# Scores between two halves of a projection, and factors between two halves of a product

## The chip, the cores and the metric

The kernel runs on one core of a Trainium2 chip. The core's engines are TensorE (PE in the profile), VectorE (DVE), ScalarE (ACT) and GpSimd (POOL), with SyncE (SP), which issues most of the DMAs. Each engine works through its own list of instructions in order and waits for the others on semaphores. The metric is the device time of one launch in microseconds, the median over several runs.

## What is computed

One decoder layer over `x` of (4, 1024, 256): a Hyena operator, cross-attention to a context of 64 rows per batch, and a gated feed-forward part with quantised weights, each followed by a residual addition and a layer norm.

```python
def hyena(u):                                   # after a projection and a depthwise convolution of 3 taps
    for n in range(2):
        y = irfft(rfft(v, n=2 * L) * rfft(h[n], n=2 * L))[..., :L]
        v = y * x[:, n]
    return v.transpose(0, 2, 1) @ w_out.T + b_out

def xattn(x_q, x_kv):                           # 16 heads of 16, 64 context rows
    q, k, v = x_q @ W_q.T + b_q, x_kv @ W_k.T + b_k, x_kv @ W_v.T + b_v
    attn = softmax(einsum('bhqd,bhkd->bhqk', qh, kh) / 4)
    return einsum('bhqk,bhkd->bhqd', attn, vh) @ W_out.T + b_out

x = layernorm(x + hyena(x))
x = layernorm(x + xattn(x, ctx))
x = layernorm(x + bitlinear(silu(bitlinear(x, w_gate)) * bitlinear(x, w_up), w_down))
```

## The kernel before

The program has two blocks, one after the other, with a barrier of all engines between them.

**The filter stage** (`hyena`) goes through the four batches. Transforms are matrix products on TensorE; for a batch `b` there are two of them, `u = 2b` and `u = 2b + 1`. For each, TensorE writes the spectrum into banks in four steps (L389, L390, L405), VectorE multiplies two banks per step by the filter (`products`, L1171 and L1172, eight steps `j` with two pairs of buffers that alternate), and GpSimd adds the real and imaginary parts into `spec_y` (`add_products`, L904 and L905; the last step is VectorE's own). A product of VectorE may overwrite its buffer once GpSimd has read what it held two steps ago (`y_ready`), and TensorE may write a bank again once VectorE has read it (`prod_done`). Then TensorE transforms back (L437, L446), and VectorE combines and gates (`level_one`, `level_two`).

The output of batch `b - 1` is finished inside batch `b`: VectorE adds the projected output to the rows (`add_residual`, L1286, in two groups of four tiles, which also gives the sums of the rows), ScalarE squares (`squares`, L780), GpSimd turns sums and squares into factors (`norm_factors`, L960 to L966: four small operations per group), ScalarE scales (`norm`, L787), and SP stores the group, waits for the store, and loads the next batch's group in its place. In the last batch `norm_factors(b - 1)` stands on GpSimd ahead of `add_products(u + 1)`. The rows of the last batch itself stay on chip (`x_tok`) and are normalised at the start of attention.

**Attention** (`attention_and_feed_forward`) works on 32 tiles of 128 rows, in chunks of 4 (`CH`). For tile `j`, TensorE makes the scores of all heads (`scores`, L1668) into `ps_score`, which has one buffer: the scores of tile `j + 1` wait until VectorE has taken the peaks (L2203) and subtracted them (`shift`, L2207) for tile `j`. ScalarE takes exponentials (L1866, two halves), TensorE turns them (`turn_prob`, L1678), ScalarE copies them out (`evac_prob`, L1872). Two tiles together give the sums of the exponentials (`sums`, L1689), VectorE's reciprocal of them (`invert`, L2214), and the weighted values (`values`, L1704). The reciprocals go through DRAM to be spread, GpSimd multiplies, and TensorE projects.

Queries of chunks 0 to 4 come from the filter stage. Those of the chunks 5, 6 and 7 (`Q_EARLY` is 5) are made among the first tiles: TensorE turns the rows (`turn_x`, L1642), ScalarE copies them (`evac_x`, L1848), TensorE multiplies by the weights (`queries`, L1650, two halves of two products into the banks `ps_ctx` and `ps_inv`), ScalarE copies them out (`evac_q`, L1853). Chunks 6 and 7 need the rows of the last batch normalised: squares on ScalarE (`squares_last`, L1839), factors and scaling on GpSimd (`norm_last`, L1984 to L1993), in two halves, after which GpSimd adds the output's bias to the chunks from chunk 0 on (`add_bias`, L2003; it waits for the chunk's rows). At tile 0 VectorE also places the values in pairs (L2187: eight additions of two operands in SBUF) and at tile 1 the keys (L2296: two multiplications of two operands in SBUF).

The order of each engine is written out by hand. TensorE's is the loop over tiles:

```python
turn_x(Q_EARLY); queries(Q_EARLY)
for j in range(TILES_ALL):
    scores(j + 1)
    if j == 2: turn_x(Q_EARLY + 2)
    turn_prob(j)
    if j == 0: turn_x(Q_EARLY + 1)
    if j in (1, 2): queries(Q_EARLY + j)
    if j % 2 == 0 and j >= 2:
        sums(j // 2 - 1)
        if j >= 4: values(j // 2 - 1)
    if j == 3: values(0)
```

## Time and profile before

| | |
|---|---|
| median of 3 runs | 682.93 us (682.90 to 683.15) |
| the profiled execution | 682.95 us, of which the span of the instructions is 681.0 us |
| busy | TensorE 96%, VectorE 90%, ScalarE 56%, GpSimd 54% of the span |
| filter stage | to 431.3 us |
| attention | 431.6 to some 556 us |
| feed-forward | to the end |
| TensorE's granted clock | full, 0.998 over the span |

A line of the timeline is one instruction or a run of equal ones: start and duration in microseconds, engine, line of the kernel, operation, what is written and read, and in brackets how long the engine had been idle before it and who released it. "PE" is a matmul, "SPq" and "POOLq" are issues of DMAs. Matmuls overlap, so the distance of two starts tells more than a duration. All times in this text count from the start of the span.

### The profile page before, as it was taken

To read this page: it belongs to the slowest core of one execution; us is meant where nothing else is said; L and a number is where in the kernel's file an instruction comes from. 1 tells how busy PE (TensorE), PEld (TensorE's weight loads), DVE (VectorE), ACT (ScalarE), POOL (GpSimd) and SP (SyncE) were. 2 spreads that over 40 slices of the span, in tenths; PEclk is the share of its full clock that TensorE was granted. 3 is DMA by queue.
4 is the path that set the end of the run, shared out by engine and by line. 5 is a ranking of instruction groups with operands and counts; after the bars stand their busy time and mean duration, and the time that the engine had idled before them with its cause. 6 is when DMAs were issued, how large, how long until landed. Compare 5 with 4: busy or idle time off the path is not lost. (4 is left out here: it accounts for less than half of the span.)

```text
span 681.0 us, 12462 instructions
## 1 busy us (share of the span) xinstructions
PE 650.6 (96%) x4284; PEld 476.8 (70%) x4284; DVE 611.0 (90%) x1241; ACT 384.5 (56%) x761; POOL 365.1 (54%) x506
## 2 busy tenths in 40 slices
PE   9999999999999999999999999888999999999996
PEld 3588765788747887568887677556777775666664
DVE  4899887999999999999999979748999979999997
ACT  3742157131368503475222634569888886888885
POOL 0633424537235753258451381284577769788786
PEclk9999999999999999999999999999999999999999
DMA  8730055230453446443743057552222221010012
GB/s 310 204 63 1 0 125 105 81 62 7 66 107 69 93 155 62 93 93 63 200 100 87 1 185 98 213 174 80 64 80 79 79 79 33 1 34 32 32 63 94
DMA packets 52680, 60.73 MB, mean 89 GB/s; under 512 B 5416, under 2 KB 46376, under 8 KB 52362
## 3 DMA queue, kind: packets, MB, share of 16 engines
q1 hardware_dynamic: 43498, 40.28, 18.3%
q0 software_dynamic: 8256, 18.86, 16.7%
q10 hardware_dynamic: 864, 0.79, 0.4%
q8 instruction: 35, 0.57, 0.3%
q14 instruction: 27, 0.22, 0.1%
HBM read 33.72 MB, written 11.53 MB: 66 GB/s over the span
## 5 line engine op out<-in xcount | busy, mean ns | idle before, releaser
L747 ACT ACTIVATE yb<-banks 128x256 f32<-128x256 f32 x64 | 24.1, 385 | 137.5 <-PE banks L446 92.3
L437 PE MATMUL banks<-inv_m,spec_y 128*128 128x256 f32 x384 | 85.5, 379 | 0.0
L473 PE MATMUL banks<-xt_in,w_in 128*128 128x512 f32 x192 | 84.5, 594 | 0.2
L437 PEld LDWEIGHTS banks<-inv_m,spec_y 128*128 128x128 f32 x384 | 73.0, 190 | 9.9
L389 PE MATMUL banks<-z_cplx,fwd_m 128*128 128x256 f32 x240 | 71.9, 381 | 3.5 <-DVE prod L1172 3.2
L390 PE MATMUL banks<-z_cplx,fwd_m 128*128 128x256 f32 x240 | 71.4, 379 | 0.0
L473 PEld LDWEIGHTS banks<-xt_in,w_in 128*128 128x128 f32 x192 | 36.1, 190 | 43.0 <-issue 40.2
L389 PEld LDWEIGHTS banks<-z_cplx,fwd_m 128*128 128x128 f32 x240 | 44.9, 190 | 11.8 <-issue 5.2
L390 PEld LDWEIGHTS banks<-z_cplx,fwd_m 128*128 128x128 f32 x240 | 45.6, 190 | 6.2
L904 POOL TENSOR_TENSOR spec_y<-prod 128x256 f32<-128x256 f32 x35 | 25.4, 726 | 42.0 <-DVE prod L1172 41.2
L2203 DVE TENSOR_REDUCE peak<-ps_score 128x16 f32<-128x1024 f32 x32 | 38.9, 1215 | 8.7 <-PE ps_score L1668 8.7
L1901 ACT ACTIVATE silu<-ps_score,gate_back 128x1024 f32<-128x1024 f32 x32 | 35.6, 1112 | 18.9 <-issue 17.6
L2253 DVE SCALAR_TENSOR_TENSOR w_raw<-ps_score,up_back,silu 128x1024 f32<-128x1024 f32 x32 | 41.0, 1280 | 1.9 <-ACT silu L1901 1.1
L1872 ACT ACTIVATE prob_t<-ps_pt 128x1024 f32<-128x1024 f32 x32 | 32.7, 1022 | 13.3 <-PE ps_pt L1678 13.3
L2207 DVE TENSOR_TENSOR prob<-ps_score,peak 128x1024 f32<-128x1024 f32 x32 | 39.2, 1224 | 1.1
L2258 DVE TENSOR_REDUCE h_peak<-w_raw 128x1 f32<-128x1024 f32 x32 | 39.0, 1220 | 1.1
L1072 DVE SCALAR_TENSOR_TENSOR z_cplx<-turned_c,sums_c 128x512 f32<-128x512 f32 x60 | 39.9, 718 | 0.0
L405 PE MATMUL banks<-z,fwd_m 128*128 128x256 f32 x168 | 38.0, 379 | 0.9 <-issue 0.9
L1866 ACT ACTIVATE prob<-prob 128x512 f32<-128x512 f32 x64 | 36.8, 622 | 1.2 <-DVE prob L2207 0.9
L2030 POOL TENSOR_TENSOR c_t<-xa_t 128x512 f32<-128x512 f32 x16 | 20.4, 1277 | 31.7 <-DMA xa_t<-inv_scratch 25.7
L405 PEld LDWEIGHTS banks<-z,fwd_m 128*128 128x128 f32 x168 | 31.8, 190 | 7.7 <-issue 3.6
L1678 PE MATMUL ps_pt<-ident,prob 128*128 128x128 f32 x256 | 34.8, 279 | 2.1 <-ACT prob L1866 2.1
(311 smaller groups left out, 1704.4 us busy)
## 6 DMA issues: line engine op xcount, KB each, us to landing
x_tok<-in_x SPq DMA_DIRECT2D x8, 512.0 KB, 4.3
x_tok<-in_b_out POOLq DMA_DIRECT2D x8, 512.0 KB, 13.9
inv_scratch<-inv_sum SPq DMA_DIRECT2D x16, 256.0 KB, 2.6
xa_t<-inv_scratch SPq DMA_DIRECT2D x16, 256.0 KB, 2.7
v_t<-left POOLq DMA_DIRECT2D x8, 511.5 KB, 5.2
x_t<-left POOLq DMA_DIRECT2D x8, 511.5 KB, 5.6
xt_in<-in_x_t SPq DMA_DIRECT2D x3, 1024.0 KB, 5.9
x_scratch<-x_tok SPq DMA_DIRECT2D x6, 512.0 KB, 4.1
```

The source lines that it names most:

```text
L389: mm(o, fwd_m[:, at + 2 * half + odd, :], zz[:, 0, :], start=True, stop=False)
L390: last = mm(o, fwd_m[:, at + 2 * half + 2 + odd, :], zz[:, 1, :], start=False, stop=True)
L405: last = mm(bank[:, half * D:(half + 1) * D], fwd_m[:, w + mt, :], z[:, src, mt, :], start=(mt == 0), stop=(mt == MT - 1))
L437: last = mm(bank[:, odd * 2 * P:(odd + 1) * 2 * P], spec_y[:, j + odd, part * D + h * P:part * D + (h + 1) * P], inv_m[:, o:o + 2 * P], st ...
L473: last = mm(proj_pair(b, t)[:, c * 512:(c + 1) * 512], w_in[:, k, TILES[t] * P:(TILES[t] + 1) * P], xt_in[:, k, c * 512:(c + 1) * 512], st ...
L1072: last = stt(z_cplx[:, g, odd], turned_c[:, slot], sign * factor, src[:, :, 0, :], ALU.mult, ALU.add)
L1866: fn(half, half, ACT.Exp, scale=DH ** -0.5).then_inc(exp_done, 1)
L1901: fn(silu[:, i % 2, :], ps_gate[:], ACT.Silu, scale=gate_back[:, i // CH % 2, i % CH:i % CH + 1])\
L2203: nc.vector.tensor_reduce(pk, sc, AX_X, ALU.max).then_inc(peaked, 1)
L2207: tt(prob[:, j % 2, :].rearrange("p (r h n) -> p r h n", r=STRIPS, n=NCTX), sc, pk.unsqueeze(3).broadcast_to([P, STRIPS, HEADS // STRIPS, ...
L2253: stt(hid[:, k, :], ps_up[:], up_back[:, i // CH % 2, k:k + 1], silu[:, i % 2, :], ALU.mult, ALU.mult)\
L2258: reduce(h_peak[:, k:k + 1], hid[:, k, :], AX_X, ALU.max, apply_absolute_value=True)\
```

## The change

There are four edits.

1. In attention, `queries` becomes `query_half(c, i)`, and TensorE's first tiles are written out without the loop: a tile's scores now stand between the two halves of each of the three projections. ScalarE's first tiles are written out to match. The first pair of tiles gets its sums after the scores of tile 5 and its values after the scores of tile 6; VectorE's first `invert` moves from behind tile 3 to behind tile 4.
2. Four of the eight squares of the last batch's rows move from attention to the end of the filter stage on ScalarE (`squares(B - 1, (0,))`, into `row_var`). GpSimd's `norm_last(0)` waits for no squares. ScalarE makes the other four around the first `evac_x`.
3. In the last batch, VectorE's `add_residual(b - 1)` is split: the first group stands ahead of `level_two(u, 1)`, the second behind it as before.
4. In the last batch, GpSimd's factors of the second group stand between the fourth and the fifth of its seven product additions, and no longer ahead of the first.

```diff
@@ ScalarE, end of the filter stage
             evac_queries(4, IB[0:2])
+            squares(B - 1, (0,))
@@ GpSimd, batch()
                 if last_one:
-                    norm_factors(b - 1)
-                add_products(u + 1)
+                    norm_factors(b - 1, (0,))
+                    add_products(u + 1, 0, 4)
+                    norm_factors(b - 1, (1,))
+                    add_products(u + 1, 4)
+                else:
+                    add_products(u + 1)
@@ VectorE, batch()
                     rotations()
+                    if last_one:
+                        add_residual(b - 1, (0,))
...
                     if last_one:
-                        add_residual(b - 1)
+                        add_residual(b - 1, (1,))
@@ TensorE, attention
-            queries(Q_EARLY)
-            for j in range(TILES_ALL):
+            query_half(Q_EARLY, 0)
+            scores(1)
+            query_half(Q_EARLY, 1)
+            turn_prob(0)
+            turn_x(Q_EARLY + 1)
+            scores(2)
+            turn_prob(1)
+            query_half(Q_EARLY + 1, 0)
+            scores(3)
+            query_half(Q_EARLY + 1, 1)
+            turn_prob(2)
+            turn_x(Q_EARLY + 2)
+            scores(4)
+            turn_prob(3)
+            query_half(Q_EARLY + 2, 0)
+            scores(5)
+            query_half(Q_EARLY + 2, 1)
+            sums(0)
+            scores(6)
+            turn_prob(4)
+            values(0)
+            sums(1)
+            values(1)
+            turn_prob(5)
+            for j in range(6, TILES_ALL):
@@ ScalarE, attention
+            squares_last(0, 2)
             evac_x(Q_EARLY)
-            squares_last(0)
-            for j in range(TILES_ALL):
+            squares_last(2, CH)
+            exponentials(0)
+            act.wait_ge(v_ready, 2 * B)
+            evac_q(Q_EARLY)
+            evac_prob(0)
+            exponentials(1)
+            evac_x(Q_EARLY + 1)
+            evac_prob(1)
+            exponentials(2)
+            evac_q(Q_EARLY + 1)
+            exponentials(3)
+            evac_prob(2)
+            evac_x(Q_EARLY + 2)
+            evac_prob(3)
+            exponentials(4)
+            evac_q(Q_EARLY + 2)
+            weight_sum(0, 0)
+            evac_prob(4)
+            evac_context(0)
+            for j in range(5, TILES_ALL):
@@ GpSimd, attention
             def norm_last(g):
-                pool.wait_ge(l_squared, CH * (g + 1))
+                if g:
+                    pool.wait_ge(l_squared, CH)
@@ VectorE, attention
+                if j == 5:
+                    invert(0)
                 shift(j)
-                if j % 2 and 3 <= j < TILES_ALL - 1:
+                if j % 2 and 5 <= j < TILES_ALL - 1:
                     invert((j - 3) // 2)
```

VectorE, attention, from the peaks of tile 3 on. Before (`peak` is a tile's reduction over the scores, `prob` its subtraction, `inv_sum` the reciprocal of a pair of tiles):

```order
L2203 TENSOR_REDUCE peak<-ps_score 128x16 [waits s_mm]
L2207 TENSOR_TENSOR prob<-ps_score,peak 128x1024 [waits pt_mm,peaked]
L2214 RECIPROCAL inv_sum<-ps_inv 128x128 [waits sum_mm]
L2203 TENSOR_REDUCE peak<-ps_score 128x16 [waits s_mm]
L2207 TENSOR_TENSOR prob<-ps_score,peak 128x1024 [waits pt_mm,peaked]
L2203 TENSOR_REDUCE peak<-ps_score 128x16 [waits s_mm]
L2207 TENSOR_TENSOR prob<-ps_score,peak 128x1024 [waits pt_mm,peaked]
L2214 RECIPROCAL inv_sum<-ps_inv 128x128 [waits inv_written,sum_mm]
L2203 TENSOR_REDUCE peak<-ps_score 128x16 [waits s_mm]
```

Now:

```order
L2230 TENSOR_REDUCE peak<-ps_score 128x16 [waits s_mm]
L2234 TENSOR_TENSOR prob<-ps_score,peak 128x1024 [waits pt_mm,peaked]
L2230 TENSOR_REDUCE peak<-ps_score 128x16 [waits s_mm]
L2234 TENSOR_TENSOR prob<-ps_score,peak 128x1024 [waits pt_mm,peaked]
L2241 RECIPROCAL inv_sum<-ps_inv 128x128 [waits sum_mm]
L2230 TENSOR_REDUCE peak<-ps_score 128x16 [waits s_mm]
L2234 TENSOR_TENSOR prob<-ps_score,peak 128x1024 [waits pt_mm,peaked]
L2241 RECIPROCAL inv_sum<-ps_inv 128x128 [waits inv_written,sum_mm]
L2230 TENSOR_REDUCE peak<-ps_score 128x16 [waits s_mm]
```

The first reciprocal moved behind the subtraction of tile 4; the second stays between tiles 5 and 6.

TensorE, attention. Before, from the second half of the last projection on (`ps_ctx<-xa_t` is a half of the projection, `ps_inv<-prob_t` the sums, `ps_ctx<-prob_t` the values, `ps_pt` turned probabilities):

```order
L1650 MATMUL ps_ctx<-xa_t,left 128x512 x2
L1689 MATMUL ps_inv<-prob_t,w_in 32x128 [waits q_evac,pt_evac]
L1689 MATMUL ps_inv<-prob_t,w_in 32x128 x15
L1668 MATMUL ps_score<-w_in,xt_in 128x128 [waits shifted]
L1668 MATMUL ps_score<-w_in,xt_in 128x128 x7
L1678 MATMUL ps_pt<-ident,prob 128x128 [waits exp_done,pt_evac]
L1678 MATMUL ps_pt<-ident,prob 128x128 x3
L1678 MATMUL ps_pt<-ident,prob 128x128 [waits exp_done]
L1678 MATMUL ps_pt<-ident,prob 128x128 x3
L1704 MATMUL ps_ctx<-prob_t,v_pairs 32x256 [waits pt_evac,v_ready,q_evac]
L1704 MATMUL ps_ctx<-prob_t,v_pairs 32x256 x7
```

Now:

```order
L1656 MATMUL ps_ctx<-xa_t,left 128x512 x2
L1695 MATMUL ps_inv<-prob_t,w_in 32x128 [waits q_evac,pt_evac]
L1695 MATMUL ps_inv<-prob_t,w_in 32x128 x15
L1674 MATMUL ps_score<-w_in,xt_in 128x128 [waits shifted]
L1674 MATMUL ps_score<-w_in,xt_in 128x128 x7
L1684 MATMUL ps_pt<-ident,prob 128x128 [waits exp_done,pt_evac]
L1684 MATMUL ps_pt<-ident,prob 128x128 x3
L1684 MATMUL ps_pt<-ident,prob 128x128 [waits exp_done]
L1684 MATMUL ps_pt<-ident,prob 128x128 x3
L1710 MATMUL ps_ctx<-prob_t,v_pairs 32x256 [waits pt_evac,v_ready,q_evac]
L1710 MATMUL ps_ctx<-prob_t,v_pairs 32x256 x7
L1695 MATMUL ps_inv<-prob_t,w_in 32x128 [waits inverted,pt_evac]
```

The scores of tile 6, the turned probabilities of tile 4 and the first pair's values now stand between the sums of the first pair and those of the second.

GpSimd, last batch of the filter stage, from the factors of the first group on. Before (`rstd` and `shift` are factors, `spec_y` the added products):

```order
L963 TENSOR_TENSOR rstd<-rstd,half_neg 128x4 [waits h_floored]
L966 TENSOR_TENSOR shift<-rstd,shift 128x4 [waits raised,h_centred]
L960 TENSOR_SCALAR rstd<-h_row_var 128x4 [waits x1_ready,h_squared]
L961 TENSOR_SCALAR shift<-h_row_sum 128x4
L963 TENSOR_TENSOR rstd<-rstd,half_neg 128x4 [waits h_floored]
L966 TENSOR_TENSOR shift<-rstd,shift 128x4 [waits raised,h_centred]
L904 TENSOR_TENSOR spec_y<-prod 128x256 [waits inv_done,prod_done]
L905 TENSOR_TENSOR spec_y<-prod 128x256
L904 TENSOR_TENSOR spec_y<-prod 128x256 [waits prod_done]
```

Now:

```order
L963 TENSOR_TENSOR rstd<-rstd,half_neg 128x4 [waits h_floored]
L966 TENSOR_TENSOR shift<-rstd,shift 128x4 [waits raised,h_centred]
L904 TENSOR_TENSOR spec_y<-prod 128x256 [waits inv_done,prod_done]
L905 TENSOR_TENSOR spec_y<-prod 128x256
L904 TENSOR_TENSOR spec_y<-prod 128x256 [waits prod_done]
L905 TENSOR_TENSOR spec_y<-prod 128x256
L904 TENSOR_TENSOR spec_y<-prod 128x256 [waits prod_done]
L905 TENSOR_TENSOR spec_y<-prod 128x256
L904 TENSOR_TENSOR spec_y<-prod 128x256 [waits prod_done]
L905 TENSOR_TENSOR spec_y<-prod 128x256
L960 TENSOR_SCALAR rstd<-h_row_var 128x4 [waits x1_ready,h_squared]
L961 TENSOR_SCALAR shift<-h_row_sum 128x4
```

The second set of four small operations moved behind four pairs of additions.

## Rows read from the trace of the kernel before

**Rows 1.** Timeline of the filter stage, VectorE and TensorE around the additions (start, duration, engine, line, operands)

```profile
377.24 0.41 DVE L1286 SCALAR_TENSOR_TENSOR x_tok<-banks,x_tok 128x256 f32<-128x256 f32 x1
377.53 1.91 PE L464 MATMUL banks<-ident,x_t 128*128 128x128 f32 x16
```

**Rows 2.** Timeline, last batch: GpSimd factors, product additions and those waiting for them

```profile
391.45 0.19 POOL L960 TENSOR_SCALAR rstd<-h_row_var 128x4 f32<-128x4 f32 x1
...
393.20 0.73 POOL L904 TENSOR_TENSOR spec_y<-prod 128x256 f32<-128x256 f32 x1
...
394.71 0.69 DVE L1171 TENSOR_TENSOR prod<-banks,spec_h 128x512 f32<-128x512 f32 x1 [2.06 <-POOL spec_y L905]
...
397.45 0.67 PE L389 MATMUL banks<-z_cplx,fwd_m 128*128 128x256 f32 x2 [0.97 <-DVE prod L1172]
...
408.78 0.42 DVE L1210 SCALAR_TENSOR_TENSOR turned_c<-banks,yc 128x256 f32<-128x256 f32 x1 [0.57 <-ACT yc L750]
```

**Rows 3.** Timeline, end of the filter stage and ScalarE around the block boundary

```profile
426.73 0.42 DVE L1286 SCALAR_TENSOR_TENSOR x_tok<-banks,x_tok 128x256 f32<-128x256 f32 x1 [0.53 <-PE banks L493]
...
431.60 0.20 ACT L1832 ACTIVATE table_of<-h_row_sum 128x1 f32<-128x1 f32 x1 [7.30 <-PEq L142]
...
433.95 0.51 ACT L1839 ACTIVATE a_spread_sq<-x_tok,h_row_sum 128x256 f32<-128x256 f32 x1
```

**Rows 4.** Timeline, first tiles of attention, VectorE, ScalarE and TensorE

```profile
435.04 2.54 DVE L2187 TENSOR_TENSOR v_pairs<-left,w_in 64x128 f32<-64x128 f32 x8
...
440.94 1.02 DVE L2296 TENSOR_TENSOR k_pairs<-left,w_in 128x384 f32<-128x384 f32 x2
...
443.89 0.57 ACT L1848 ACTIVATE xa_t<-ps_ctx 128x512 f32<-128x512 f32 x1
...
445.00 1.98 PE L1650 MATMUL ps_ctx<-xa_t,left 128*128 128x512 f32 x4 [0.31 <-ACT xa_t L1848]
...
446.82 1.88 PE L1650 MATMUL ps_inv<-xa_t,left 128*128 128x512 f32 x4
...
449.43 1.23 DVE L2203 TENSOR_REDUCE peak<-ps_score 128x16 f32<-128x1024 f32 x1 [4.17 <-PE ps_score L1668]
...
450.69 1.22 DVE L2207 TENSOR_TENSOR prob<-ps_score,peak 128x1024 f32<-128x1024 f32 x1
...
456.22 0.96 DVE L2214 RECIPROCAL inv_sum<-ps_inv 128x128 f32<-128x128 f32 x1 [4.31 <-PE ps_inv L1689]
```

**Rows 5.** Timeline, tiles 4 to 6 of attention, TensorE and VectorE

```profile
461.07 1.09 PE L1678 MATMUL ps_pt<-ident,prob 128*128 128x128 f32 x8 [0.78 <-ACT prob L1866]
...
462.09 1.08 PE L1689 MATMUL ps_inv<-prob_t,w_in 128*32 128x128 f32 x32
...
462.99 1.05 PE L1704 MATMUL ps_ctx<-prob_t,v_pairs 128*32 128x256 f32 x16
463.24 0.96 DVE L2214 RECIPROCAL inv_sum<-ps_inv 128x128 f32<-128x128 f32 x1 [0.39 <-PE ps_inv L1689]
...
464.76 1.22 DVE L2203 TENSOR_REDUCE peak<-ps_score 128x16 f32<-128x1024 f32 x1 [0.56 <-PE ps_score L1668]
```

**Rows 6.** Costliest groups of the page (busy, mean ns, idle before): exponentials, turned probabilities

```profile
L1872 ACT ACTIVATE prob_t<-ps_pt 128x1024 f32<-128x1024 f32 x32 | 32.7, 1022 | 13.3 <-PE ps_pt L1678 13.3
...
L1866 ACT ACTIVATE prob<-prob 128x512 f32<-128x512 f32 x64 | 36.8, 622 | 1.2 <-DVE prob L2207 0.9
```

**Rows 7.** Timeline of GpSimd and VectorE: products with and without company

```profile
414.78 2.37 POOL L939 TENSOR_TENSOR v_t<-yq,x_odd 128x1024 f32<-128x1024 f32 x1 [7.23 <-DVE yq L1246]
...
416.06 1.23 DVE L1186 TENSOR_TENSOR sums_c<-turned_c 128x128 f32<-128x128 f32 x1
```

**Rows 8.** Timeline of GpSimd in attention: second half of the rows, then biases

```profile
443.03 0.20 POOL L1984 TENSOR_SCALAR l_rstd<-l_var 128x4 f32<-128x4 f32 x1 [2.13 <-ACT a_spread_sq L1839]
...
447.07 2.35 POOL L2003 TENSOR_TENSOR x<-x,w_in 128x1024 f32<-128x1024 f32 x1
```

**Rows 9.** DMA issues from 431 to 437 us: rows of the stream (count, size, median us to landing)

```profile
x<-x_scratch SPq DMA_DIRECT2D x3, 512.0 KB, 4.9
```

More of the change, by code:

```diff
@@ L770, in squares @@
                     act.wait_ge(act_seq, GROUPS * G_OUT * (b + 1) + 1)
-                for g in range(GROUPS):
+                for g in groups:
                     for t in range(G_OUT):
@@ L896, in add_left, with add_products @@
                     .then_inc(conv_done[slot(b, t)], 16)
[L898 to L899 removed]
+            def add_products(u, j0=0, j1=BANKS - 1, first=False, prod=prod):
+                for j in range(j0, j1):
                     pool.wait_ge(prod_done, 8 * u + j + 1)
```

82 lines of the change are left out of this document (29 added, 53 removed).

## The prediction

> **What bounds the kernel now.** I read the busy shares first. TensorE and VectorE are both busy for nine tenths of the span, so no single engine is the bound, and only a place where one waits for the other can pay. I then read the timeline at the places that the diff touches. In the last batch of the filter stage, VectorE stands 2.06 us behind GpSimd's product additions, and TensorE has to wait for VectorE right after [rows 2]. In attention, VectorE stands 4.17 us before the peaks of tile 3 and 4.31 us before its first reciprocal [rows 4]. From tile 6 on it stands for half a microsecond per tile [rows 5], so attention is paced by the loop of scores, peaks and subtraction, and whatever moves tile 6 moves the end of the kernel by as much. So I price two things: when attention starts, and when VectorE takes the peaks of tile 6, at 464.76 before.
>
> **The additions (edit 3)** bring and cost nothing. VectorE is busy without a gap there and does the same work. The first group's four additions, 1.4 us, now delay the gating, which ended at 377.2. TensorE turned the gated rows from 377.53 on [rows 1], but it came from earlier projections, not from waiting, and its last quarter starts 1.4 us later still. Bounds: 0 to +0.1.
>
> **The factors (edit 4).** The second group's four operations take 393.20 - 391.45 = 1.75 us [rows 2]. Without them the first additions start 1.7 us sooner, and so does VectorE's third product, which stood 2.06 us. What TensorE gets is less. Its last quarter of the transform waited 0.97 us for that product [rows 2]; beyond that it is limited by its own matmuls. With the slower first matmul after a wait I take 1.1 us. The 1.75 us come back on GpSimd behind the fourth step, where VectorE's last three products need them. That eats VectorE's own lead, but VectorE has slack behind it: it waits 0.57 us for ScalarE in front of the second and again of the third bank of the back transform [rows 2], and both waits hang on TensorE. From there TensorE is busy up to the end of the block. So the block ends 1.1 us sooner, between 0 and 1.3. The normalised second group is stored some 4 us later. Behind that store stand SP's loads of the last rows and of the weights of attention, and GpSimd's bias DMA. None of the waits at the end of the block was on a DMA: VectorE waited for TensorE's banks [rows 3]. So I price this at nothing and keep it as a rival.
>
> **The squares (edit 2).** Four squares of 0.51 us with the reading of the sum come to some 2.6 us on ScalarE. They can start with the first additions, at 426.73, and ScalarE was idle for 7.30 us ahead of the boundary [rows 3]; they are done at some 430, a microsecond before VectorE. In attention ScalarE loses four squares. Two of the others precede the first copy of the turned rows, which is late by 0.1 us. The price is nothing. But GpSimd's factors now start at 431.9, not behind squares.
>
> **The first tiles (edit 1), worked out in the clock of before.** The second set of four squares, some 2.4 us, is gone from between the probabilities of tile 0 and the exponentials of tile 1, so that the copies of the turned rows of chunk 6 start at some 441.55, not 443.89. The first half projection follows 445.00 - 443.89 = 1.11 later, at 442.7, and the scores of tile 3 stand behind one half, 446.82 - 445.00 = 1.82 later, at 444.5. The peaks start some 0.8 after them, at 445.3, and not at 449.43 [rows 4]: 4.1 us gained at tile 3. Then the chain runs on: subtraction 1.26 later (450.69 - 449.43), exponentials another 1.26 later at 447.8, on ScalarE 1.04 of exponentials, 0.97 for the turned probabilities (both overlap a little with what follows) [rows 6], 1.11 for the copies of chunk 7, on TensorE half a projection (1.82), scores (some 0.65), the other half (1.81), and the first sums start at 455.2. The reciprocal starts 463.24 - 462.09 = 1.15 after them [rows 5], at 456.4, against 456.22 [rows 4]. It is as late as before, but with four tiles subtracted behind it and one more: tile 5 is subtracted at 458.5 to 459.7. A whole tile is gained.
>
> It is given back at the next reciprocal. VectorE's second reciprocal still stands ahead of the peaks of tile 6. It waits for the second sums, and these now stand on TensorE behind the scores of tile 6 (which wait for VectorE's subtraction of tile 5), the turned probabilities of tile 4 and the first pair's values. From the end of that subtraction: 0.07 to release, 0.65 of scores, 462.09 - 461.07 = 1.02, 0.98 of values (a run of 1.05) and 1.15, together 3.9 us [rows 5] in which VectorE does nothing. The reciprocal starts at 463.6, the peaks of tile 6 0.9 later, at 464.46. That is 0.3 us sooner than before, not 4.
>
> **What GpSimd now collides with.** Two rows show a price for company: while GpSimd multiplies for 2.37 us from 414.78, a VectorE operation with both operands in SBUF takes 1.23 us, up to GpSimd's end [rows 7]; that is 417.2, and for 128 columns, where two key products of 384 columns take 1.02 us together [rows 4]. VectorE's eight value additions (2.54 us from 435.04) and two key products (1.02 us) are of this form. Before, GpSimd was waiting for squares or at operations on four columns then. Now its factors and scalings start at 431.9. A half takes 447.07 - 443.03 = 4.04 us [rows 8], so two of its four scalings lie beside the first value additions, and I take 0.95 us for VectorE's two waits. The two halves end at 431.9 + 8.1 = 440.0, with GpSimd's own waits 440.6, and then the bias of chunk 0 follows at once, since its rows land at some 437 (an issue at 432 and 4.9 us [rows 9]). It takes 2.35 us, to 443.0 [rows 8]. VectorE's key products come due at 441.1, and so wait until 443.0. The peaks of tile 2 start at 444.05, those subtracted at 446.5, the scores of tile 3 at 446.55 and not at 444.5. The chain from there on has no slack, so tile 6 is at 464.46 + 2.05 = 466.5: 1.75 us later than before.
>
> The Trainium skill, "SBUF — State Buffer", section "Who interferes with whom", says that a VectorE instruction with two SBUF inputs and a GpSimd instruction that reads SBUF exclude each other: the one that issues second is blocked until the first has ended. The row of 1.23 us agrees with it, and it speaks against this change: with it attention is 1.75 us slower, without it 0.3 us faster.
>
> **The sum.** 682.95 of the profiled execution (0.02 above the median) - 1.1 + 1.75 = 683.6 us.
>
> **The rivals.**
>
> *No block at the key products.* The two times are only half a microsecond apart. If the products come first or GpSimd is late, only the value additions cost, 0.75 us at tile 3: 682.95 - 1.1 + 0.45 = 682.3. Without any company 682.95 - 1.1 - 0.3 = 681.55. For it speaks that GpSimd's start may slip behind VectorE's clearing of `v_pairs`.
>
> *The gap at the second reciprocal does not open* (it hangs on my reading of the order alone) and the tile gained at 458 stays: 464.76 - 462.1 = 2.7 us, less 2.05: 682.95 - 1.1 - 0.65 = 681.2, and 679.1 if nothing collides either. Against it speaks that both waits are written in the order above.
>
> *Slower: the filter stage gives nothing.* Mechanism: the second group's rows are stored some 4 us later, and the bias DMA of the last batch, which is queued behind store and load, lands after VectorE's additions to the second group want it at 428. It decides from 4 to 5 us of delay on. Then the block ends where it did, and 682.95 + 1.75 = 684.7. If instead chunk 1's rows are there when the bias of chunk 0 ends, the second key product is blocked again, by 2.35: 682.95 - 1.1 + 4.1 = 685.95.
>
> **How the numbers follow.** Forecast 0.46; no block at the key products 0.24, of which half lies at 681.55 or below; no gap at the reciprocal 0.08; no gain in the filter stage 0.14; a second block 0.08. The predicted time is 683.6. The range leaves out the very fast end and the second block: 681.2 to 685.2. A measurement tells some 0.2% (1.37 us) from no change: faster than 681.56 in 0.12 + 0.08 = 0.20, slower than 684.3 in 0.14 + 0.08 = 0.22, the rest 0.58.
>
> **What the profile after would show.** Factors of the second group beside the fifth product and TensorE without its 0.97 us; attention starting at 430.5; scores of tile 3 some 4 us, or only 2, sooner against that start; a gap of 3.9 us ahead of VectorE's second reciprocal; key products stretched to more than 2 us beside a GpSimd addition. I am wrong if the key products keep their 1.02 us, if the gap isn't there, or if VectorE waits for a bias at the end of the filter stage.

## The result, and the profile after

The changed kernel takes 685.91 us (median of 5 runs, 685.88 to 686.43) against 683.13 us (682.90 to 683.18) for the kernel before on the same chip: a ratio of 1.0045, with a 95% interval from 1.0034 to 1.0056. By the medians it is slower by 2.8 us; by the ratio, and by the spans of the two profiled executions, by 3.0, the figure that I use below. I had forecast 683.6, with a range up to 685.2.

The page of the kernel after: the span is 3.0 us longer, and the costliest groups of attention have the durations of [rows 6] to 2 ns, and what grew is idle time (for ScalarE's copies of the turned probabilities, below, 19.8 us where it was 13.3).

```profile
span 684.0 us, 12450 instructions
...
L1891 ACT ACTIVATE prob_t<-ps_pt 128x1024 f32<-128x1024 f32 x32 | 32.8, 1024 | 19.8 <-PE ps_pt L1684 12.8
```

**End of the filter stage**, where [rows 2] and [rows 3] stood. The timeline of VectorE, SP and TensorE, and the DMA issues between 396 and 420 us (count, size, median us to landing):

```profile
393.06 0.69 DVE L1175 TENSOR_TENSOR prod<-banks,spec_h 128x512 f32<-128x512 f32 x1 [0.40 <-POOL spec_y L905]
...
401.23 0.36 SPq L312 DMA_DIRECT2D x_scratch<-x_tok  x1
...
404.55 0.51 SPq L341 DMA_DIRECT2D spec_h<-x_scratch  x1
...
415.75 1.07 PE L560 MATMUL banks<-ident,spec_h 128*128 128x128 f32 x8 [1.11 <-DMA spec_h<-x_scratch]
```

```profile
x_tok<-in_b_out POOLq DMA_DIRECT2D x2, 512.0 KB, 12.9
...
spec_h<-x_scratch SPq DMA_DIRECT2D x1, 512.0 KB, 11.1
```

The same load in the kernel before: its issue, TensorE's first use of the rows, and its time to landing:

```profile
402.51 0.51 SPq L342 DMA_DIRECT2D spec_h<-x_scratch  x1
...
415.67 1.04 PE L561 MATMUL banks<-ident,spec_h 128*128 128x128 f32 x8
```

```profile
spec_h<-x_scratch SPq DMA_DIRECT2D x1, 512.0 KB, 5.0
```

VectorE's third product starts 1.65 us sooner and stood only 0.40 us. TensorE's 0.97 us are gone, and it reaches its back transform 1.2 us sooner. But the second group's rows are now stored at 401.23, and the load of chunk 4's rows, which SP issues behind that store, leaves at 404.55 and travels 11.1 us. TensorE stands 1.11 us for exactly these rows at 415.75, and the block ends when it ended before: VectorE's clearing of `v_pairs`, the first thing it does in attention, starts at 431.98 us (431.87 before).

**First tiles of attention**, in the places of [rows 4]: timeline of VectorE, GpSimd and TensorE.

```profile
435.15 3.08 DVE L2214 TENSOR_TENSOR v_pairs<-left,w_in 64x128 f32<-64x128 f32 x8
...
440.54 2.36 POOL L2030 TENSOR_TENSOR x<-x,w_in 128x1024 f32<-128x1024 f32 x1
440.79 2.99 DVE L2325 TENSOR_TENSOR k_pairs<-left,w_in 128x384 f32<-128x384 f32 x2
...
446.23 0.73 PE L1674 MATMUL ps_score<-w_in,xt_in 32*128 32x128 f32 x16 [1.17 <-DVE prob L2234]
...
447.02 1.23 DVE L2230 TENSOR_REDUCE peak<-ps_score 128x16 f32<-128x1024 f32 x1 [0.85 <-PE ps_score L1674]
...
451.53 1.23 DVE L2230 TENSOR_REDUCE peak<-ps_score 128x16 f32<-128x1024 f32 x1 [2.02 <-PE ps_score L1674]
...
458.27 0.96 DVE L2241 RECIPROCAL inv_sum<-ps_inv 128x128 f32<-128x128 f32 x1 [4.25 <-PE ps_inv L1695]
459.14 1.16 DVE L2230 TENSOR_REDUCE peak<-ps_score 128x16 f32<-128x1024 f32 x1
```

**Tiles 4 to 6**, in the places of [rows 5], and the granted clock (PEclk) in stretches around them:

```profile
461.62 0.73 PE L1674 MATMUL ps_score<-w_in,xt_in 32*128 32x128 f32 x16 [3.42 <-DVE prob L2234]
...
462.27 1.60 PE L1684 MATMUL ps_pt<-ident,prob 128*128 128x128 f32 x8
...
463.81 1.94 PE L1710 MATMUL ps_ctx<-prob_t,v_pairs 128*32 128x256 f32 x16
...
465.52 1.34 PE L1695 MATMUL ps_inv<-prob_t,w_in 128*32 128x128 f32 x32
...
466.94 0.96 DVE L2241 RECIPROCAL inv_sum<-ps_inv 128x128 f32<-128x128 f32 x1 [5.38 <-PE ps_inv L1695]
...
467.82 1.16 DVE L2230 TENSOR_REDUCE peak<-ps_score 128x16 f32<-128x1024 f32 x1
```

```profile
core 0: us, PE busy (x) PEld busy (x) DVE busy (x) ACT busy (x) POOL busy (x), PEclk, DMA share, GB/s
458.00:461.60 3.60, 0.20 (x8) 0.00 (x0) 3.26 (x3) 0.95 (x2) 0.00 (x0) 1.00 0.27 77
461.60:465.00 3.40, 3.38 (x36) 2.34 (x40) 0.00 (x0) 0.00 (x0) 0.00 (x0) 0.66 0.26 77
465.00:468.00 3.00, 2.42 (x52) 1.63 (x48) 1.06 (x2) 2.13 (x4) 0.47 (x1) 0.81 0.00 0
```

VectorE takes the peaks of tile 3 2.4 us sooner than before, and those of tile 4 5.6 us sooner. ("Tile 3 peaks" is short for this from here on.) Part of that is given back at the first reciprocal, which has moved between tiles 4 and 5 and waits 4.25 us for its sums: tile 5 peaks at 459.14, 1.2 us sooner. The rest, and 3.1 us more, is lost at the second reciprocal, ahead of which VectorE stands idle for 5.38 us: TensorE waited 3.42 us for VectorE's tile 5, and then ran transpose, values and sums at a granted clock between 0.5 and 1.0, in 1.60, 1.94 and 1.34 us where [rows 5] have 1.09, 1.05 and 1.08.

From here on I count from the start of that clearing of `v_pairs`. The moment at which attention starts differs by up to 1.6 us between profiled executions of kernels with one and the same filter stage, and most of the difference, up to 1.4 us, is there by 42 us of the program; so for the filter stage I take the stretch from the issue of the first store of the last batch to the start of attention. It is 38.37 us before (from 393.50) and 38.47 after (from 393.51). Counted from the start of attention, tile 6 peaks 2.94 us later than before, tile 8 3.36 us, and the kernel ends 2.85 us later (a step of 0.3 us in the feed-forward part is there in some kernels and not in others).

### The profile page after: what moved, and what is told of

It reads as the page before. It is cut to its first block and busy times, and to the rows that moved or that the text cites. A ratio compares the mean times of both kernels' runs of the same rounds, so it can differ in the third digit from the quotient of the medians.

```text
span 684.0 us, 12450 instructions
## 1 busy us (share of the span) xinstructions
PE 650.9 (95%) x4268; PEld 477.4 (70%) x4284; DVE 612.9 (90%) x1241; ACT 385.0 (56%) x761; POOL 365.9 (53%) x506
## 5 line engine op out<-in xcount | busy, mean ns | idle before, releaser
L1891 ACT ACTIVATE prob_t<-ps_pt 128x1024 f32<-128x1024 f32 x32 | 32.8, 1024 | 19.8 <-PE ps_pt L1684 12.8
```

## The experiments

All numbers of this table but the last column are from one profiled execution each, in microseconds against the kernel before: where attention starts, and, counted from there, the peaks of tiles 3, 6 and 8 and the end. The last column is the ratio of times with its interval.

| kernel | start | tile 3 | tile 6 | tile 8 | end | ratio |
|---|---|---|---|---|---|---|
| the change | +0.11 | -2.52 | +2.94 | +3.36 | +2.85 | 1.0045 (1.0034 to 1.0056) |
| split | +0.91 | 0 | 0 | 0 | -0.28 | 0.9997 (0.9987 to 1.0006) |
| split_rows | -1.21 | 0 | 0 | 0 | -0.38 | 0.9976 (0.9968 to 0.9985) |
| rows_only | +0.43 | 0 | 0 | 0 | -0.28 | 0.9997 (0.9988 to 1.0006) |
| no_split | -0.11 | -2.52 | +2.94 | +3.34 | +3.06 | 1.0048 (1.0030 to 1.0065) |
| gap_busy | +0.77 | -2.55 | +1.28 | +1.94 | +1.78 | 1.0034 (1.0021 to 1.0047) |
| bias_late | +0.53 | -3.77 | +1.62 | +2.28 | +2.32 | 1.0054 (1.0042 to 1.0067) |
| bias_busy | +0.18 | -3.76 | +0.06 | +0.73 | +0.78 | 1.0012 (1.0003 to 1.0021) |
| after_rows | -0.68 | -2.52 | +4.25 | +4.23 | +3.77 | 1.0042 (1.0030 to 1.0054) |
| rows_busy | -1.75 | -2.54 | +1.29 | +1.96 | +1.89 | 1.0012 (1.0003 to 1.0021) |
| adds_back | +0.32 | -2.52 | +1.31 | +1.98 | +1.51 | 1.0046 (1.0032 to 1.0059) |
| adds_busy | +0.29 | -2.55 | +1.27 | +1.94 | +1.73 | 1.0036 (1.0022 to 1.0050) |
| squares_back | +0.89 | -1.08 | +5.52 | +5.66 | +5.62 | 1.0078 (1.0066 to 1.0091) |
| squares_busy | -0.03 | -1.68 | +2.15 | +2.81 | +2.70 | 1.0055 (1.0043 to 1.0068) |
| fill | +0.54 | -2.51 | -2.03 | -2.06 | -2.48 | 0.9967 (0.9956 to 0.9979) |
| inv_late | +0.85 | -2.55 | -5.76 | -1.54 | -1.69 | 0.9985 (0.9975 to 0.9994) |
| all_mended | -0.13 | -3.77 | -6.99 | -2.77 | -2.82 | 0.9943 (0.9931 to 0.9956) |
| exp_early | -1.77 | -3.77 | -6.98 | -3.02 | -3.04 | 0.9932 (0.9920 to 0.9945) |
| exp_scores | -0.28 | -3.75 | -6.97 | -2.73 | -3.19 | 0.9941 (0.9927 to 0.9954) |

### The filter stage: why its gain did not arrive

**split.** The kernel before with the fourth edit alone.

```diff
@@ GpSimd, batch()
                 if last_one:
-                    norm_factors(b - 1)
-                add_products(u + 1)
+                    norm_factors(b - 1, (0,)); add_products(u + 1, 0, 4)
+                    norm_factors(b - 1, (1,)); add_products(u + 1, 4)
```

> The kernel before with the change's fourth edit alone (GpSimd's factors of the two groups apart, four additions between them). Theory, rows late: the second group's store is issued 4.4 us later, the load of the late queries' rows behind it lands after TensorE wants it, and TensorE waits 1.1 us for it at the end of the batch: the attention block starts at 431.7 us as in both kernels, the time is that of before within 0.2 us (683.1). Rival, the split works and the gain is lost by the squares and additions of the other edits: the block starts 1.1 us sooner, the time is 682.0 us.

Ratio 0.9997: no gain. TensorE and SP in its timeline:

```profile
405.16 0.51 SPq L342 DMA_DIRECT2D spec_h<-x_scratch  x1
...
416.55 1.07 PE L561 MATMUL banks<-ident,spec_h 128*128 128x128 f32 x8 [1.30 <-DMA spec_h<-x_scratch]
```

The wait on `x_scratch`'s rows is there without any other edit. Its start of attention is 0.9 us later than before's, of which 0.6 us are there at the first store already; from there to attention it takes 38.66 us.

**split_rows.** The same, and SP issues the load of chunk 4's rows when the first group's store has landed, which is all that it reads.

```diff
@@ SP, out_groups(b)
                     sp.wait_ge(st_x1, 16 * (i + 1))
                     load_group(b + 1, g)
+                    if b == B - 2 and g == 0:
+                        load_rows(4)
...
-            for c in range(4, Q_EARLY):
-                load_rows(c)
```

> The kernel before with the fourth edit and, besides, the load of the rows of chunk 4 issued right behind the store of the first group, which is all it reads, ahead of the store of the second. Theory, rows late: TensorE no longer waits for the rows, the attention block starts 1.1 to 1.2 us sooner (430.5), the time is 682.0 us. Rival: another thing falls due at the same place (the bias additions, the convolution rows of the last batch), the block starts at 431.6 and the time is 683.1.

The rows in its timeline, on SP:

```profile
396.82 0.51 SPq L339 DMA_DIRECT2D spec_h<-x_scratch  x1
```

The second store still leaves 4.4 us later, at 401.21, but the rows have left ahead of it. Ratio 0.9976: 1.6 us faster than before. TensorE has no wait on a DMA left in the last batch, and from the first store to attention it takes 37.17 us, 1.2 less than before.

**rows_only**, the control: the kernel before with that edit of SP's order alone.

> The kernel before with only the load of the rows of chunk 4 moved up behind the store of the first group; GpSimd's factors as before, not split. In the kernel before TensorE did not wait for these rows. Theory, split and rows pay only together: the same as before, 683.1 us within 0.6. Rival, the earlier load pays by itself (1.6 us with the split): 681.5 us, and the split is worth nothing.

Ratio 0.9997, and 38.38 us from the first store to attention. The earlier load is worth nothing by itself, and neither is the split: only together do they pay. Both sides of my pricing stand here. The split was worth what I said (1.1 us forecast, 1.2 in the trace, 1.6 by the ratio), and it was held back by a load that I had called free.

### Attention: order, company and clock

**no_split.** The changed kernel with the fourth edit taken back.

> The changed kernel with the fourth edit taken back (edits 1 to 3 alone). Theory: the whole loss is the attention order's, since the filter stage gave nothing: 3.0 us over before, 686.0 us, TensorE's idle before the scores of tile 6 is 3.4 us, the key product takes 3.0 us. Rival: the loss depends on where the filter stage's transfers and clock leave the block, and without the split the time falls toward 684 us.

Ratio 1.0048. The whole loss is attention's: the block is the changed kernel's to 0.02 us up to tile 8.

**gap_busy.** The changed kernel, with matmuls that nothing reads in TensorE's idle time.

```diff
@@ TensorE, attention
             sums(0)
+            pe.wait_ge(pt_evac, 4)
+            for n in range(24):
+                transpose(ps_pt[:, n % PAIRS * P:(n % PAIRS + 1) * P], ident[:], ident[:])
             scores(6)
```

> The changed kernel with 24 transposes of the identity, read by nothing, put into TensorE's idle time between the sums of pair 0 and the scores of tile 6; the order of all other work is as it was, and the scores still wait for VectorE's tile 5. Theory, the lower clock after the idle time costs by itself: with TensorE busy the granted clock stays at 1.0 in 461.6 to 468 us (0.66 and 0.81 in the changed kernel), transpose, values and sums take 1.09, 1.05 and 1.08 us again (1.60, 1.94, 1.34), tile 6 peaks 1.5 us sooner, the time is 684.4 us. Rival, those matmuls are slow for another reason (operands late, transfers): their durations stay, and the time is 685.9 us.

Its timeline (TensorE and VectorE) and the clock:

```profile
458.76 2.84 PE L1801 MATMUL ps_pt<-ident 128*128 128x128 f32 x24
...
462.90 1.09 PE L1684 MATMUL ps_pt<-ident,prob 128*128 128x128 f32 x8
...
463.92 1.07 PE L1710 MATMUL ps_ctx<-prob_t,v_pairs 128*32 128x256 f32 x16
...
464.81 1.06 PE L1695 MATMUL ps_inv<-prob_t,w_in 128*32 128x128 f32 x32
...
465.93 0.96 DVE L2244 RECIPROCAL inv_sum<-ps_inv 128x128 f32<-128x128 f32 x1 [3.75 <-PE ps_inv L1695]
```

```profile
461.60:465.00 3.40, 2.76 (x48) 2.13 (x52) 0.59 (x1) 0.00 (x0) 0.00 (x0) 1.00 0.43 115
465.00:468.00 3.00, 2.18 (x51) 1.33 (x44) 2.04 (x2) 2.88 (x5) 1.23 (x1) 1.00 0.00 0
```

The clock stays at 1.00, the three steps take 1.09, 1.07 and 1.06 us, the reciprocal stands 3.75 us where I had forecast 3.9, and tile 6 peaks 1.66 us sooner than in the changed kernel. The order of work is the changed kernel's, so this part of the loss is the clock's. The ratio fell by 0.0011, some 0.8 us; the intervals of the two ratios overlap, and the traces carry this verdict more than the times do.

**bias_late.** The changed kernel, with GpSimd's bias addition of chunk 0 behind VectorE's key products.

```diff
@@ GpSimd, add_bias(c)
+                if c == 0:
+                    pool.wait_ge(k_ready, DT)
```

> The changed kernel with GpSimd's bias addition of chunk 0 behind VectorE's key products, on which it waits. Theory, the two exclude each other: the key products take 1.0 us and not 3.0, tile 2 peaks 2 us sooner; TensorE then is the later one (it was idle only 1.2 us before the scores of tile 3), so tile 6 peaks 1.2 us sooner, 684.7 us. Rival, nothing of the 2 us reaches tile 6, since TensorE's order up to the second reciprocal sets it: 685.9 us. Second rival, the whole 2 us: 683.9 us.

In its timeline, VectorE's products and tile 2, TensorE's scores of tile 3 and transpose of tile 4:

```profile
441.20 1.01 DVE L2327 TENSOR_TENSOR k_pairs<-left,w_in 128x384 f32<-128x384 f32 x2
...
442.13 1.22 DVE L2232 TENSOR_REDUCE peak<-ps_score 128x16 f32<-128x1024 f32 x1
...
445.40 0.73 PE L1674 MATMUL ps_score<-w_in,xt_in 32*128 32x128 f32 x16
...
461.87 1.97 PE L1684 MATMUL ps_pt<-ident,prob 128*128 128x128 f32 x8
```

The key products take 1.01 us, not 2.99, and tile 2 peaks 2.0 us sooner; tile 3 only 1.25 us, since TensorE no longer waits there. Tile 6 peaks 1.3 us sooner, as the theory had it. In the time nothing of this is to be seen (1.0054 against 1.0045, inside the intervals). The clock was low here too: the transpose of tile 4 took 1.97 us. The times of this kernel went from 685.69 to 687.43 us, the two highest in executions with a mean clock of 0.993. The other three, at 0.997, average 686.0 us, and so do the five of the changed kernel.

**bias_busy.** Both edits at once.

> The changed kernel with both: the bias addition of chunk 0 behind the key products, and the 24 unread transposes in TensorE's idle time. With the bias addition alone the block was 1.3 us sooner at tile 6, with the transposes alone 1.7 us, and TensorE's clock was lower for longer in the first (0.60, the transpose of tile 4 took 1.97 us). Theory, both costs are real and the clock hid part of the first: tile 6 peaks 2.9 us sooner than in the changed kernel counted from the block's start, the block is 2.4 to 2.6 us shorter, 683.5 us. Rival, the two overlap: no more than 1.7 us sooner, 684.5 us or more.

Tile 6 peaks 2.88 us sooner than in the changed kernel (1.66 and 1.25 add to 2.91), and the ratio is 1.0012. So company and clock are two costs that add, and against gap_busy (1.0034) the company is worth 1.0 us at the end of the trace and 1.5 us by the ratios. That bias_late alone shows none of it in its times is explained only in part by the lower clock of two of its five executions. The profiled one of the other three has a block 0.5 us shorter than the changed kernel's and an attention that starts 0.4 us later; the other two have no trace.

**after_rows.** The changed kernel with the rows of chunk 4 loaded sooner (the edit of split_rows).

> The changed kernel with only the load of the rows of chunk 4 moved up. Theory: the 1.1 us of TensorE's wait come off in the filter stage and the attention block stays as it is, 3.0 us longer than before's: 684.8 us. Rival: the block's start moves the transfers against the attention block and it gives the 1.1 us back: 685.9 us.

**adds_back.** The changed kernel with the third edit taken back.

> The changed kernel with its third edit taken back: both groups' additions stand together again behind the second product. Forecast and theory: no difference, 685.9 us within 0.6. Rival: additions apart hold TensorE's banks or delay the store of the first group by up to 1 us, 685.0 us.

Neither gave what its theory said of the traces. The first stretch is after_rows, the second adds_back, each with TensorE behind the same idle time and the clock:

```profile
460.82 1.24 PE L1675 MATMUL ps_score<-w_in,xt_in 32*128 32x128 f32 x16 [3.42 <-DVE prob L2235]
461.99 1.97 PE L1685 MATMUL ps_pt<-ident,prob 128*128 128x128 f32 x8
```

```profile
458.00:461.60 3.60, 0.78 (x12) 0.78 (x16) 2.73 (x3) 0.16 (x2) 0.00 (x0) 0.81 0.25 73
461.60:465.00 3.40, 3.40 (x32) 2.33 (x28) 0.00 (x0) 0.00 (x0) 0.00 (x0) 0.50 0.26 77
465.00:468.00 3.00, 2.86 (x52) 1.89 (x48) 0.54 (x1) 2.05 (x4) 0.39 (x1) 0.65 0.00 0
```

```profile
461.82 0.73 PE L1672 MATMUL ps_score<-w_in,xt_in 32*128 32x128 f32 x16 [3.42 <-DVE prob L2232]
462.48 1.09 PE L1682 MATMUL ps_pt<-ident,prob 128*128 128x128 f32 x8
```

```profile
461.60:465.00 3.40, 3.18 (x64) 2.55 (x68) 0.17 (x1) 0.30 (x1) 0.00 (x0) 1.00 0.27 80
```

The idle time is 3.42 us in both, as in the changed kernel. In after_rows the clock is low from ahead of the first matmul on and for most of the stretch, and tile 6 comes 1.3 us later than in the changed kernel; in adds_back it is not low at all, and tile 6 comes 1.6 us sooner. In after_rows and adds_back attention's order is the changed kernel's, so what the idle time costs is not set by the order alone, and it differs between executions of one kernel. The six executions of adds_back show this: with a mean clock of 0.999 they took 684.66 and 685.34 us, with 0.996 685.57 to 686.70, with 0.993 687.89. All five executions of the changed kernel had 0.995 or 0.996.

What the edits themselves are worth can therefore be told only with the clock held up. The next three kernels have the unread transposes of gap_busy and are to be compared with it (1.0034).

**rows_busy.**

> The changed kernel with the rows of chunk 4 loaded sooner and with the 24 unread transposes in TensorE's idle time. With the rows alone the filter stage gained 0.8 us in the profiled execution, and the clock then was at 0.5 for twice as long behind the idle time (460.4 to 467.0 us), 0.9 us more than in the changed kernel's. Theory, the two are independent and the clock hid the rows' gain: 1.1 us under the kernel with the transposes alone (1.0034 of before), so 1.0018 of before, 684.2 us. Rival, the rows gain nothing ahead of the changed block: 685.3 us.

Ratio 1.0012, 1.5 us under gap_busy, with a block that is as long to 0.1 us, and 37.16 us from the first store to attention. The rows' gain reaches the end of the changed kernel too. In after_rows the stretch is 37.17 us as well, and the clock had hidden the gain in the times.

**adds_busy.**

> The changed kernel with the third edit taken back and the transposes in the idle time, so that the clock does not blur it. Theory: the third edit is worth nothing, 1.0034 of before as with the transposes alone, 685.3 us within 0.5. Rival: the additions apart cost what the profiled execution of adds_back lacked, 684.2 us.

Ratio 1.0036 against 1.0034, with a block as long to 0.1 us: the third edit is worth nothing that these intervals, some 1 us to either side, could show.

**squares_back**, and **squares_busy**. The second edit taken back: eight squares in attention, four ahead of the exponentials of tile 0 and four of tile 1.

```diff
@@ ScalarE
-            squares(B - 1, (0,))
...
-            squares_last(0, 2)
             evac_x(Q_EARLY)
-            squares_last(2, CH)
+            squares_last(0)
...
             evac_prob(0)
+            squares_last(1)
             exponentials(1)
```

> The changed kernel with its second edit taken back: all eight squares in the attention block, GpSimd's factors start behind the first four. Theory, the early start of GpSimd is what brings its passes against VectorE's products: the value products take 2.5 us again and not 3.1, the key products 1.0 and not 3.0, but the rows of chunk 6 come 1.3 us later to TensorE and ScalarE does 2.8 us more ahead of tile 2: the block within 1.0 us of the changed kernel's, 685.0 to 686.5 us. Rival, without the collisions the order pays: 684 us or less. Rival, ScalarE's squares cost more than they save: over 687 us.

> The changed kernel with the second edit taken back and the transposes in the idle time. Theory: without the early squares the rows of chunk 6 come late to TensorE, tile 3 peaks 1.4 us later than in the changed kernel, and this stays: 1.0055 of before, 686.7 us; the rest of what squares_back lost (2.3 us at tile 8) was the longer low clock. Rival: the whole 2.3 us stay with TensorE busy, 1.0068 of before, 687.6 us.

I was wrong on the first, by more than its slower rival: 1.0078. As expected the collisions lessen (value products 2.54 us, key products 1.10). But TensorE turns the rows of chunk 6 ahead of the scores of tile 2, in every one of these orders, so that when the rows come late, the scores do. In the kernel before it waited for them too (first stretch). With the new order it comes to that place sooner and waits longer (second stretch, squares_back, with the peaks of tile 2):

```profile
440.96 0.66 PE L1642 MATMUL ps_ctx<-ident,x 128*128 128x128 f32 x4 [1.46 <-POOL x L1993]
```

```profile
442.53 1.12 PE L1647 MATMUL ps_ctx<-ident,x 128*128 128x128 f32 x4 [2.10 <-POOL x L2019]
...
445.74 1.23 DVE L2229 TENSOR_REDUCE peak<-ps_score 128x16 f32<-128x1024 f32 x1 [3.61 <-PE ps_score L1673]
```

And the clock was low there too (1.12 us for a run that takes 0.66) and again behind tile 5. squares_busy has only the second of these places filled. Its ratio is 1.0055, the 0.0021 (1.4 us) over gap_busy that I had expected, but that is not a price at full clock. Its profiled execution, the only one with a mean clock of 0.998, took 685.62 us, and there tiles 3, 6 and 8 and the end are each 0.9 us later than in gap_busy. The other four have 0.995 and took 686.96 to 687.53 us; where their clock was low no trace shows. So the second edit, given the first, is worth some 0.9 us at full clock, and more where the clock falls. The 0.9 us are less than what the squares take on ScalarE's side: with them (squares_busy) its copies of the turned rows of chunk 6 start at 443.90 us, without them (the changed kernel) at 441.97, but in the latter 1.17 us of that lead are lost where TensorE waits ahead of the scores of tile 3.

### Mending it

**fill.** TensorE's order at tile 6 changed, no work added: what can run while VectorE shifts tile 5 stands ahead of the scores that wait for it.

```diff
@@ TensorE, attention
             sums(0)
-            scores(6)
             turn_prob(4)
             values(0)
             sums(1)
+            scores(6)
             values(1)
```

> The changed kernel with TensorE's order at tile 6 altered: transpose of tile 4, values of pair 0 and sums of pair 1 ahead of the scores of tile 6, not behind them. Theory, gap before the second reciprocal: all three can run while VectorE shifts tile 5, so TensorE is not idle for 3.4 us, its matmuls there take 1.1 us each and not 1.3 to 1.9 us, the reciprocal starts at 461.6 and not at 466.9, tile 6 peaks at 462.6 and not at 467.8: up to 5 us sooner; what follows may take some of it back, so 681.0 to 683.5 us. Rival, the loss is made earlier, at the products of values and keys (2.5 us): the time stays within 1.5 us of the changed kernel, 684.5 us or more.

In its timeline, the scores of tile 6 and their peaks:

```profile
462.05 0.73 PE L1674 MATMUL ps_score<-w_in,xt_in 32*128 32x128 f32 x16 [0.52 <-DVE prob L2234]
...
463.28 1.16 DVE L2230 TENSOR_REDUCE peak<-ps_score 128x16 f32<-128x1024 f32 x1
```

Ratio 0.9967: faster than the kernel before by 2.3 us, with the company and the late rows still in it. The gap was the change's undoing. And it is the order that pays, not only the clock: with the gap filled by unread work tile 6 came 1.66 us sooner (gap_busy), and here, where the sums of the second pair no longer stand behind VectorE's tile 5, it comes 4.97 us sooner.

**inv_late.** VectorE's first two reciprocals one tile later, TensorE's order as in the change.

```diff
@@ VectorE, loop over tiles
-                if j == 5:
-                    invert(0)
                 shift(j)
+                if j in (5, 6):
+                    invert(j - 5)
...
-                if j % 2 and 5 <= j < TILES_ALL - 1:
+                if j % 2 and 7 <= j < TILES_ALL - 1:
```

> The changed kernel with VectorE's first two reciprocals one tile later each: the first behind the shift of tile 5, the second behind that of tile 6; TensorE's order untouched. Theory, the wait moved: tile 5 is shifted at 455.3 and not at 459.1, TensorE goes from the sums to the scores of tile 6 without a pause at 458.2, tile 6 peaks at 459.1 and not at 467.8, no low clock; ScalarE, with the weight sums, then bounds it, and some 5 of the 8.7 us are left: 681.0 us, between 679.5 and 682.5. Rival, the loss sits at the products of values and keys and the reciprocals cover it: over 684.5 us.

In its timeline, the peaks of tiles 6 and 7:

```profile
459.85 1.16 DVE L2230 TENSOR_REDUCE peak<-ps_score 128x16 f32<-128x1024 f32 x1
...
466.10 1.23 DVE L2230 TENSOR_REDUCE peak<-ps_score 128x16 f32<-128x1024 f32 x1 [2.47 <-PE ps_score L1674]
```

Tile 6 peaks at 459.85, 8.7 us sooner from the block's start, as expected. Of that 4.9 us are left at tile 8: tile 7's scores stand behind the first pair's evacuated values, and the next transpose behind ScalarE's exponentials. The time is 682.1 by its ratio, 1.1 us over the expectation.

**all_mended.** The two waits mended (reciprocals, rows) and the bias addition behind the key products.

> The changed kernel with three mends: reciprocals one tile later, the bias addition behind the key products, the rows of chunk 4 loaded right behind the store they read. If the three add up: 681.0 less 1.1 for the rows and up to 1.2 for the products, 678.8 us; if ScalarE is the bound after the reciprocals moved, the 1.2 us of the products is lost: 679.9 us.

Ratio 0.9943, or 679.2 us, between the two expectations. In the trace the block is 1.13 us shorter than in inv_late, and the filter stage takes 37.16 us from the first store on: the mends add up.

**exp_early, exp_scores.** Besides, ScalarE's exponentials of tile 5 ahead of its first weight sum; and, in the second, TensorE's scores of tile 7 and transpose of tile 5 ahead of the values of pair 1.

> The three mends, and ScalarE's exponentials of tile 5 ahead of its first weight sum, where it was idle for 2.1 us. Theory: ScalarE sets the pace behind tile 6 (the scores of tile 8 waited 1.3 us for its exponentials); 1.1 us of its work goes into its idle time, so tile 8 peaks about 1 us sooner, 677.9 us. Rival, TensorE's wait for the evacuated values (0.8 us) sets it: 678.9 us, no gain.

> The same, and TensorE's scores of tile 7 ahead of the values of pair 1 and the transpose of tile 5 ahead of them too. Theory: VectorE, idle 2.5 us before tile 7, is fed sooner, ScalarE gets tile 7 without a pause: up to 2 us over exp_early in tile 7, half of it left behind it, 676.9 us. Rival, ScalarE is full from 461 us on in either order: the same as exp_early.

Ratios 0.9932 and 0.9941, neither to be told from all_mended. At tile 8 they peak 0.25 us sooner and 0.04 us later than all_mended. In exp_early TensorE's transpose of tile 6 still waits 1.07 us for ScalarE, in exp_scores 2.24 us (that line in both timelines):

```profile
463.26 1.09 PE L1685 MATMUL ps_pt<-ident,prob 128*128 128x128 f32 x8 [1.07 <-ACT prob L1886]
```

```profile
465.05 1.08 PE L1685 MATMUL ps_pt<-ident,prob 128*128 128x128 f32 x8 [2.24 <-ACT prob L1887]
```

Tile 7 was 2.5 us sooner in the second and lost it at once: ScalarE is the pace there, as exp_scores' rival had it. exp_early has the lowest ratio: 4.6 us under the kernel before, 7.7 under the change.

## Why the prediction was wrong

The forecast was 682.95 - 1.1 + 1.75 = 683.6. In the same terms the profiled execution reads 682.95 + 0.11 (start of attention) + 1.78 (order and company at full clock, the end in gap_busy) + 1.07 (clock) = 685.9. So the second term, 1.75, was met, the first was not there, and the third was missing. The clock's term is the difference of two traces at their ends; at tile 6 it is 1.66, and the two ratios give 0.8.

**The sentence that failed first** is "None of the waits at the end of the block was on a DMA ... So I price this at nothing". I had read that the store moves back by 4 us and that SP's loads stand behind it, and then looked for waits on a DMA in the trace of before only. A transfer that lands just ahead of its use shows no wait. The load left at 402.51 and needed 5.0 us before; TensorE came to the rows at 415.67. With the change it left at 404.55 and needed 11.1 us: 2.0 us later on the queue, but 8.1 at its landing, and now behind the issue of GpSimd's bias DMA (512 KB) and no longer ahead of it. Whether that DMA is what made the transfer long was not tried by itself. I kept the case as a rival with 0.14, with the bias itself as the late transfer and 684.7 as its time; the effect was as I wrote, the transfer another.

**The second step** is the gap before the second reciprocal. That it opens, and why, was right; I summed 0.07 + 0.65 + 1.02 + 0.98 + 1.15 = 3.9 us from [rows 5], and it measures 3.75 with the clock at 1.00. The step that failed is that I took these durations from a stretch in which TensorE had been busy, and put them behind 3.4 us in which it does nothing. The change's own execution paid 5.38. My forecast had the idle time in it, on VectorE's side, and I did not ask what TensorE would do in it.

**Company.** The value products took 3.08 us, 0.54 more (forecast 0.95), the key products 2.99, 1.97 more (forecast 2.05), up to the end of GpSimd's addition, as described. The Trainium skill, "SBUF — State Buffer", section "Who interferes with whom", has this rule, and the runs agree: without the addition beside them the products took 1.01 us. But I wrote that "the chain from there on has no slack". It has 0.7: TensorE waited 1.17 us for tile 2, and of the 1.97 us only 1.25 reach tile 3 (bias_late), and 1.2 tile 6 (bias_busy against gap_busy). The products came second by only 0.25 us (440.79 against 440.54), where I had half a microsecond.

**Sizes that met by luck.** Without the key products' company and at full clock tile 6 is 0.06 us later than before (bias_busy), where my rival without that block had 0.45; with it 1.28, where I had 1.75; and to tile 8 another 0.66 us are lost, of which I had nothing. At the end this makes 1.78. That it is next to my 1.75 is chance: 0.4 us too much for the order, 0.1 too much for the company, and 0.5 us behind tile 6 that I did not have.

**Edits 2 and 3.** The additions cost nothing that the runs could show, as forecast. Of the squares I priced the cost apart, at nothing, and booked their gain under the first tiles: "some 2.4 us, is gone", so that the copies of chunk 6 start at 441.55 (they start at 441.97). Taken back, the squares cost 0.9 us at full clock. So that gain is part of the change and of my sum. But only some of the 2.4 us counts, since TensorE then waits for VectorE's tile 2.

**The rivals.** No block at the key products and no gap at the reciprocal: both refuted by the rows. The second block of a key product did not happen either: the bias of chunk 1 starts at 448.19, 5.29 us after that of chunk 0 has ended, waiting for its rows. It gave 685.95, next to the result, for a reason that isn't there.

## What to carry to other kernels

When an edit delays a store, follow each load queued behind it to its reader, and compare landing and use; that the trace shows no wait there says only that there was a margin, not how large. When an order opens idle time on TensorE, do not price what stands behind it by durations from a busy stretch, and look first for work in the queue that can go into the gap: three steps moved ahead of one wait turned a loss of 3.0 us into a gain of 2.3. And compare small edits with such a gap filled: as long as it is open, it costs between 0 and 3 us by execution, more than they are worth.

## What the runs showed of the hardware

The clock behind one and the same idle time of 3.42 us was at 1.00 in one execution, at 0.50 (1.2 GHz of 2.4) from inside the next transpose up to the sums in another, and already ahead of the scores and up to the second values in a third; tile 6 moved by up to 2.9 us with it, between adds_back and after_rows. I had not expected it to differ between kernels whose work there is the same. The Trainium skill, "TensorE: Matmul & The Clock Gate", section "Part 1: The HAM clock gate", says that the gate knows two rates, half and full, and chooses by how busy the engine has been. The windows agree as to the two rates: 1.00 in some, 0.50 in others, and values between these only where it changes within the window. Filling the idle time with matmuls that nothing reads kept the full one in the profiled executions of all five kernels in which it was so filled; of squares_busy four more executions, without a trace, had a lower mean clock (0.995).
